# Twenty unread 16-bit products at the end of TensorE's program in both dense blocks

## The reference

```python
x = _L0_conv_ref(x, ...)                 # window attention, 12 heads, then a dense block:
#   m = gelu(layernorm(x) @ mlp_w1 + mlp_b1) @ mlp_w2 + mlp_b2 ; x + m      (96 -> 384 -> 96)
x = _L1_conv_ref(x, ...)                 # norm, 96 -> 192, 3x3 depthwise conv, scans, norm, 192 -> 96,
#   then a dense block of the same form as above
t = t + _L2_attn_ref(_ln_t(t), ...)      # full attention, 8 heads of 48
t = t + _L2_ffn_ref(_ln_t(t), ...)       # two layers with sign weights and an absmax scale
t = t + _L3_attn_ref(_ln_t(t), ...)      # causal attention, 6 heads
t = t + _L3_ffn_ref(_ln_t(t), ...)       # 4 experts, the best 2 of each token
```

## Time and profile before

| | |
|---|---|
| median of 3 runs | 1188.33 us (1187.22 to 1189.34) |
| the profiled execution | 1182.08 us |
| its span, first to last instruction | 1180.2 us |
| TensorE busy | 1049.2 us, 89% of the span |
| mean granted TensorE clock | 0.960 of full speed |
| VectorE, ScalarE, GpSimd busy | 58%, 49%, 44% |

### The profile page before, as it was taken

One profiled execution on the slowest core, in us unless ns is written; L12 is line 12 of the kernel. 1 busy time (PEld: TensorE's weight loads), 2 busy tenths in 40 slices (PEclk: granted clock), 3 DMA queues, 4 the chain that ended last, 5 costly groups with the idle time before them and its releaser, 6 DMA issues. The chain is left out here.

```text
span 1180.2 us, 28488 instructions
## 1 busy us (share of the span) xinstructions
PE 1049.2 (89%) x11009; PEld 690.4 (58%) x11009; DVE 679.2 (58%) x1872; ACT 583.8 (49%) x1335; POOL 515.3 (44%) x678
## 2 busy tenths in 40 slices
PE   4999999799979799699999987888898978999998
PEld 2677655477745466477677654455455444466665
DVE  3899834588834375356566673684556566333333
ACT  1667633366633366366656652545343422365654
POOL 4766564666465354554554436244001000345442
PEclk9999999899989899899999997897999999899999
DMA  6400000000000000000000000000000000000000
GB/s 125 91 2 2 2 2 1 1 1 2 1 2 1 1 1 1 1 2 2 1 1 1 2 1 1 1 2 1 1 2 2 2 1 1 1 9 15 9 15 14
DMA packets 28383, 9.59 MB, mean 8 GB/s; under 512 B 26530, under 2 KB 28257, under 8 KB 28257
## 3 DMA queue, kind: packets, MB, share of 16 engines
q1 hardware_dynamic: 25232, 6.95, 2.8%
q10 hardware_dynamic: 3024, 0.92, 0.4%
HBM read 6.29 MB, written 1.57 MB: 7 GB/s over the span
## 5 line engine op out<-in xcount | busy, mean ns | idle before, releaser
L1080 POOL TENSOR_TENSOR fa_e<-fa_e,fa_rc 128x1024 f32<-128x1024 f32 x64 | 120.8, 1897 | 142.6 <-DVE fa_rc L1302 142.5
L1236 ACT ACTIVATE fa_e<-bank,fa_nm 128x256 f32<-128x256 f32 x256 | 118.5, 495 | 2.3 <-DVE fa_nm L1296 2.3
L137 PE MATMUL bank<-hT,e_w 96*64 96x512 f32 x384 | 91.0, 609 | 0.0
L2101 ACT ACTIVATE ex_G<-bank,e_b 128x512 f32<-128x512 f32 x96 | 64.4, 687 | 49.8 <-PE bank L137 47.1
L164 POOL TENSOR_TENSOR ln_v<-MV,eps 128x2 f32<-128x2 f32 (+3 forms) x81 | 16.2, 200 | 163.0 <-DVE MV L201 90.0
L2173 DVE SCALAR_TENSOR_TENSOR X<-bank,ex_L,X 128x96 f32<-128x96 f32 x128 | 31.7, 310 | 91.6 <-PE bank L137 85.1
L1296 DVE TENSOR_REDUCE fa_nm<-bank 128x4 f32<-128x1024 f32 x64 | 75.2, 1216 | 12.2 <-PE bank L1105 12.2
L2004 POOL TENSOR_TENSOR ex_tmp<-e_b,ex_L 128x384 f32<-128x384 f32 x8 | 6.7, 833 | 169.3 <-DVE ex_L L2161 169.3
L1823 ACT ACTIVATE ca_e<-bank 128x768 f32<-128x768 f32 x48 | 38.9, 810 | 78.1 <-PE bank L1632 78.1
L1905 DVE TENSOR_REDUCE ca_z<-bank 128x2 f32<-128x256 f32 x96 | 48.8, 550 | 49.7 <-PE bank L1632 49.6
L137 PEld LDWEIGHTS bank<-e_w,ex_G 128*64 128x64 f32 x1536 | 67.2, 137 | 17.2 <-issue 10.5
(11 more groups left out here) (249 smaller groups left out, 2515.4 us busy)
## 6 DMA issues: line engine op xcount, KB each, us to landing
out_tokens<-X SPq DMA_DIRECT2D x8, 192.0 KB, 2.1
X<-in_x SPq DMA_DIRECT2D x14, 96.0 KB, 3.4
e_w<-in_L_ffn_w SPq DMA_DIRECT2D x2, 576.0 KB
bias0r<-in_L_conv_rpb_table ACTq DMA_DIRECT2D x16, 24.0 KB
m0w<-in_L_conv_mlp_w SPq DMA_DIRECT2D x2, 144.0 KB
m1w<-in_L_conv_w SPq DMA_DIRECT2D x2, 144.0 KB
f_w<-in_L_ffn_W SPq DMA_DIRECT2D x2, 142.5 KB
mixer<-in_mixer SPq DMA_DIRECT2D x1, 256.0 KB
```

Of the source, the lines that this page charges most:

```text
L137: last = pe.matmul(out[columns], weights[:, columns], moving, **flags)
L1080: pool.tensor_tensor(e, e, r.broadcast_to([P, 4, TOK]), ALU.mult).then_inc(s["nrm"], 1)
L1236: last = act.activation(E[v % 4][:, i, c, :], bank[b + i][:, c * TOK:(c + 1) * TOK], ACT.Exp, bias=NM[v % 4][:, i, c:c + 1], accum_out=SU[ ...
L2101: act.activation(G[e % 2][:, j, :], bank[(KH * e + j) % NB][:], ACT.Gelu, bias=k.eb1[:, e, j:j + 1]).then_inc(s["gelu"], 1)
```

## The change

Both calls of `mlp` share one function, so the one added line acts at the end of `ml0` and at the end of `ml1`. It issues twenty products into bank 0. In the last step the gelu reads banks 3 to 5, so bank 0 is free.

```diff
                 pairs(pe, steps, body)
                 down(steps - 1, 1)
+                keep_warm(pe, k, bank[0], 20)
 
             @block.scalar
```

## The result

| | before | after |
|---|---|---|
| median | 1185.07 us (1181.89 to 1189.42, 22 runs) | 1188.88 us (1184.23 to 1192.78, 22 runs) |
| profiled execution | 1182.08 us | 1188.76 us |

The ratio is 1.0026 with a 95% interval of 1.0014 to 1.0039, which is +3.1 us (+1.7 to +4.6) on 1185. The change makes the kernel slower by about a quarter of a per cent. The ratio goes by the 22 runs as a whole, whose means lie 3.1 us apart, while the two medians lie 3.8 apart. The kernel before is itself 3.3 us faster here than in the three runs shown ahead of the prediction. In what follows, a ratio is turned into microseconds on 1185.

The account below looks back on a forecast made before the run. Bound at both ends: VectorE arrives last at the barrier, TensorE about 2.1 us earlier, then idling into half clock. 2.40 + 2.35 - 0.6 + 0.2 - 0.6 = +3.8, giving 1192.1 us, range 1189.0 to 1194.3.

Parts of the forecast that it names:

- I put the same shift on it: Whole kernel: the runs' median stood 6.25 us above the profiled execution; adding this to 1185.9 gave 1192.1 us.
- the whole gain at one end and the estimate at the other: Both ends: full clock gain at one, the estimated gain at the other, said to sum to +1.2 to +2.4 us.
- A: Both ends: the barrier moves by 4.3 to 4.8 us, the clock returns part; +2.5 to +6.6, slower, chance 0.67.
- The barrier waits for the products: Both ends: as at window attention's end, GpSimd starts only after the products are through, though nobody reads their bank.
- Rival D: Both ends: the barrier does not wait for unread products; -3.3 us, 1185.0, faster, chance 0.04.
- Its price: Both barriers: twenty products take 4.29 us, GpSimd follows 0.76 later, so it starts 2.40 (`ml0`) and 2.35 (`ml1`) later.
- The clock behind `ml0`: First widening behind `ml0`: probably still at full clock, at most 0.95 us back, 0.6 taken; the clock falls afterwards.
- hidden behind VectorE's: Behind `ml0`'s first widening: TensorE's own taps run at half clock, as now, covered by VectorE's taps.
- The 0.2 for a slower mixing: First mixing behind `ml0`: it comes closer to the clock's fall; at most 1.8 us lost, 0.2 taken.
- The clock behind `ml1`: Projections behind `ml1`: the clock most likely falls, somewhat later against them; 0 to 3.2 us back, 0.6 taken.
- Rival C: Later stretches, such as 813 to 829: their clock changes; -3.8 us or 1184.5 possible, chance 0.05 of ending faster.
- Rival B: Both ends: the clock holds; +0.65 us, 1189.0, no change that can be told, chance 0.24.

Follow-up runs that it names:

- ScalarE in TensorE's place: Kernel before, without products, ScalarE running six unread gelu copies behind the last `down` at both ends: 1189.63 us, ratio 1.004.
- all three kernels: Kernel before with products in idle time: at `ml1` only 0.9978; with eight at `ml0` too 0.9983; with those and 13 in `conv_mixer` 0.9981.

## Why the prediction was right and wrong

The direction and the size of the change were right: +3.8 forecast, +3.1 measured. The time, 1188.88 us, lies 0.12 below the range's low end of 1189.0. **The step that failed is "I put the same shift on it"**, the shift being put on the 1188.33 of three runs. The profiled execution stood 6.25 below that median "with no row to say why", and this should have widened the range downward. The executions of the kernel before spread from 1181.89 to 1189.42, and the three runs lay in the upper part. What the runs showed in its place: over 22 runs the median is 2.99 above the first profiled execution, not 6.25, and executions of one kernel differ by where and how long the clock is at half. On the 1185.07 of 22 runs the same +3.8 gives 1188.9.

That this comes so close to 1188.88 is partly luck: the terms behind the barrier were off by 1.1 to 1.4 us each, in opposite ways. Behind `ml0` 1.5 came back by the end of `ml1` where 0.4 was forecast, behind `ml1` 1.95 where 0.6 was, and 1.4 that the forecast had not was lost, if it was, behind the first scores. One sum of the prediction is wrong by itself: "the whole gain at one end and the estimate at the other" gives, with the whole gain at `ml0`, 4.8 - 0.95 - 0.6 = 3.2 and not 2.4, so it lies inside A.

Point by point:

- **The barrier waits for the products.** Shown by the changed kernel, by 8, 20 and 60 products, and by ScalarE in TensorE's place. Rival D falls. Later work waits for the barrier, so the time follows it: +0.5, +3.1 and +23.6 us with 8, 20 and 60 products, and +4.7 with ScalarE late.
- **Its price.** Forecast 2.40 and 2.35, measured 2.29 and 2.25. The two parts were off in opposite ways: the products end 4.43 behind the last `down` and not 4.29, and GpSimd starts 0.51 behind them and not 0.76.
- **The clock behind `ml0`.** The widening was at full clock in three of four profiles (2.07 in the third), worth 0.95, and TensorE's taps fell to half clock as forecast. But the 0.6 taken for it did not reach the first mixing: its statistics came 18.97 to 19.23 behind the last `down` in all four profiles, against 16.68 or 16.69 in three of before, and 18.58 in the fourth, where the mixing took 2.93 at half clock. The way over the second image, which waits for GpSimd, was as long as the way over VectorE's taps (before, ScalarE's fill of that grid ends at 222.16 + 1.31 = 223.47, just ahead of L979), and the forecast followed only the latter. TensorE's taps and second widening lie on that way, so their half clock is not "hidden behind VectorE's". The execution with the widening at 2.07 shows it: its statistics came no later, at 18.98. The 0.2 for a slower mixing did not come either; the mixing stayed at 1.57 in all four.
- **And further on.** Of these 2.4 only 0.8 are left at the end of `ml1`. The executions with products spent less of the stretch at half clock, 18 us on average against 26. Right behind `ml0` that is plain, since the clock held for 8 to 9 us behind the last `down` in place of 2 to 5 (6 in the execution with the slow widening). Why less of it was at half further on as well was not settled, and may be chance of a few executions. The forecast had no term for it.
- **The clock behind `ml1`.** I took 0.6 of at most 3.2. It gave 1.5 in the first profile and 1.95 on average. "The clock most likely falls here too, somewhat later against the projections" came out in three of six executions (5.36 for the projections). In the other three it held until they had ended. Half clock in the first groups of the attention, some 20 to 23 us behind the last `down`, followed in the five executions of these twelve whose scores came at 12.05 to 12.25, two of them of the kernel before, and in none of the seven whose scores came later. So a gain at the scores can be lost there, with or without products.
- **Rival C**, that a later stretch changes its clock, describes the single profiled pair: 6.7 us apart, of which 2.5 arise behind `ml0`, 0.79 behind `ml1` and 4.3 behind the first scores, less the 0.86 by which the changed kernel's execution was ahead at `ml0`'s end. In the last column this pair has 90 against 68 us at half clock. Such differences happen in both kernels; that they favour one of them was not shown.
- **Rival B** (the clock holds at both ends) happened in none of the four executions of the changed kernel, but it did at one end at a time: at the widening in three, and through the projections in the third, which took 3.67, the sign for which the prediction calls its clock step wrong. Products in idle time at `ml1` held the clock in all three kernels and brought the scores 3.15 ahead of the first profile of before.

## What to carry to other kernels

Filler for the clock is free only as long as another engine's work covers it, at a barrier too: look for who arrives last, and how long before it TensorE is done (here 2.1 us, room for 8 products of 0.216 us and not for 20). Put the rest behind the barrier, where TensorE waits anyway. Follow the clock through the next idle stretches as well, in more than one execution, since it may fall there instead, and take the base of a forecast from more than a few executions when one of them stands apart.

## What the runs showed of the hardware

An execution's clock is not a fixed property of the program. The same instructions up to `ml0`'s end took 207.51 to 212.04 us in different executions, the longer ones with 3 or 7 us of it at half clock, and the first widening of the kernel with products at `ml1` only took 2.08 in one profile and 1.52 in the other. Behind both dense blocks GpSimd's first work came 0.5 to 0.6 us behind the last engine's work, whether VectorE, TensorE or ScalarE came last: at `ml0` 0.53 behind VectorE before, 0.51 behind TensorE after, and 213.10 - (208.64 + 3.94) = 0.52 behind ScalarE. At the end of window attention it was 0.76 behind TensorE's last product, which is why the forecast put this gap too high here.
